# Two sixteen-head cross attentions of a four-layer decoder: the shift of the softmax from the leading bf16 parts, in row tiles

## The chip, the cores and the metric

The kernel runs on one core of a Trainium2 chip. The metric is the device time of one launch in microseconds (us). Every time below comes from the timed runs of the kernel before or from one profiled execution of it.

## The reference

A decoder of four layers works on `x` of shape (2, 512, 256), with a context of shape (2, 1024, 256). Each layer is self attention (or a recurrence, or retention), cross attention and a feed-forward part. The change concerns the cross attentions of layers 2 and 3, with 16 heads of 16 features, 512 queries and 1024 keys:

```
def _L2_xattn_ref(query, key, value, ..., key_padding_mask, attn_mask, Wq, bq, Wk, bk, Wv, bv, Wo, bo):
    ...
    scores = jnp.einsum('bhtd,bhsd->bhts', q, k) * scale
    scores = scores + attn_mask[None, None, :, :]
    scores = jnp.where(pad, -jnp.inf, scores)
    ...
    probs = jax.nn.softmax(scores, axis=-1)
    out = jnp.einsum('bhts,bhsd->bhtd', probs, v)
    return out @ Wo.T + bo
```

Layer 3 is the same without masks and biases. The mask of layer 2 is one (512, 1024) matrix of floats for all heads and both batch elements.

## The kernel before

The program is a row of stages, each with its own buffers, semaphores and a block for each engine; a stage begins when the one before has ended on all engines. `a2x` is the attention of layer 2, `a3x` that of layer 3; both call `narrow_attention_stage` (L2067). A projection stage ahead has written q and k to DRAM in three bf16 parts each (leading, middle, rest), whose sum has nearly the precision of float32.

The work goes by units: one batch element and a group of four heads, eight units in a stage. In a unit the six products of the parts are stacked to 96 contraction rows (`STACK`), so that one bf16 matmul gives scores of nearly float32 precision. The unit has two parts:

- *Chunks.* For each query tile of 128, each head and each half of the keys, one matmul (L2257) gives a 128x512 chunk in PSUM, of which VectorE takes the maximum over the keys: a plain reduction in a3x (L2400), in a2x a reduction that adds the float32 mask on the way (L2403). These are 32 chunks a unit, with two PSUM buffers of 512 (`chunk`). The maxima are reduced (L2421), turned by TensorE (L2268), split in three bf16 parts by VectorE (L2426 to L2433) and placed by DMA in three further contraction rows of q (L2204), beside three rows of ones in k.
- *Jobs.* For each tile of 128 keys and two heads, scores turned (keys on the partitions) minus the maximum come into `scores_T` (L2279), two buffers of 1024. In a2x, even key tiles get the mask by three bf16 matmuls against the identity (L2283), odd ones by an addition on VectorE into `masked` (L2412). ScalarE takes the exponential (L2379), TensorE multiplies with the values and a column of ones in column tiles of 32 (L2307) into `u`. At the unit's end ScalarE copies `u` (L2381), TensorE turns it (L2339) and VectorE divides (L2447, L2450).

The order on TensorE is written out by hand: chunks of the next unit (and ten of the one after) stand between the jobs of this one. Units run in loops over the head groups (`Fori`, L2235, L2354, L2384, L2462), two units in a turn. SyncE issues all loads in the order of its program. The stage `a0x` (`wide_attention_stage`, L457), which the change leaves alone, has eight heads of 64: its rows (L582) are two matmuls of 64 contraction rows each, with one reduction over 1024 elements (L726). `mask_stage` (L2822) prepares the mask parts and the padding row ahead of a2x.

## Time and profile before

| | us |
|---|---|
| median of 3 timed runs | 2957.84 (2949.81 to 2963.62) |
| profiled execution, its time | 2966.22 |
| its span, first to last instruction | 2964.4 |
| stage a2x | 393.75 |
| stage a3x | 261.99 |

The windows view, the first of the rows below that has stages, gives for each stretch its length, then the busy time of each engine with its number of instructions, TensorE's granted clock as a share of full speed, the busy share of the DMA engines and GB/s. The span is what the trace shows; 1.8 us of the execution lie outside it. A busy share counts the time in which an engine has an instruction under way. Matmul records overlap, as matmuls are pipelined: a 512-column matmul at full clock has a record of some 0.38 us and is followed by the next after 0.22.

### The profile page before, as it was taken

How to read it: one execution, taken by the hardware profiler on the slowest of the kernel's cores; microseconds unless marked ns; L12 is line 12 of the kernel's file. 1: busy time of each engine (PE TensorE's matmuls, PEld its weight loads, DVE VectorE, ACT ScalarE, POOL GpSimd, SP SyncE). 2: the span in 40 equal slices, each digit the busy share in tenths (PEclk: the TensorE clock that was granted, in tenths of full speed). 3: DMA queues.
4: the chain of work that ended last, by engine and by line, in shares of the span. 5: the costliest groups of instructions: out<-in, count | busy, mean ns of one | idle time of the engine just before them, and what ended most of it. 6: DMA issues, size and time to landing. Idle time of an engine off the chain costs nothing. (4 is left out here: it accounts for less than half of the span.)

```text
span 2964.4 us, 35664 instructions
## 1 busy us (share of the span) xinstructions
PE 2215.4 (75%) x11958; PEld 1048.9 (35%) x11958; DVE 1564.5 (53%) x2826; ACT 944.7 (32%) x1311; POOL 610.5 (21%) x540
## 2 busy tenths in 40 slices
PE   4778788897547766799567487887799693688854
PEld 2343322224424444555335122223444332322222
DVE  3543343425659998221433576674344425477757
ACT  2341133342224544122213133334110201345544
POOL 1000044440249999000101200000000101200013
PEclk8888899998768999799788699999899756789976
DMA  4502511100270500010441631200110000543000
GB/s 145 141 12 107 175 41 49 36 11 15 81 147 12 83 1 2 22 43 21 122 114 37 148 88 24 47 15 1 32 32 27 32 1 0 161 92 69 15 1 15
DMA packets 161134, 164.08 MB, mean 55 GB/s; under 512 B 14946, under 2 KB 131404, under 8 KB 160716
## 3 DMA queue, kind: packets, MB, share of 16 engines
q1 hardware_dynamic: 161000, 162.37, 21.3%
q8 instruction: 74, 1.21, 0.2%
q14 instruction: 60, 0.49, 0.1%
HBM read 108.97 MB, written 53.02 MB: 55 GB/s over the span
## 5 line engine op out<-in xcount | busy, mean ns | idle before, releaser
L2403 DVE CUSTOM_DVE_ANT_0 a2x_chunk<-a2x_chunk,mask 128x512 f32<-128x512 f32 x256 | 173.7, 703 | 80.9 <-PE a2x_chunk L2257 69.5
L726 DVE TENSOR_REDUCE a0x_row_most<-a0x_rows 128x2 f32<-128x1024 f32 x88 | 107.8, 1225 | 165.3 <-PE a0x_rows L582 165.3
L2400 DVE TENSOR_REDUCE a3x_chunk_maxima<-a3x_chunk 128x1 f32<-128x512 f32 x256 | 166.6, 689 | 40.4 <-PE a3x_chunk L2257 38.1
L1115 ACT ACTIVATE a1x_exp<-a1x_scores 128x1024 f32<-128x1024 f32 x128 | 124.1, 1021 | 174.9 <-PE a1x_scores L1046 174.9
L783 POOL TENSOR_TENSOR x_stream<-x_stream,feature_rows 128x256 f32<-128x256 f32 x40 | 27.9, 734 | 655.9 <-SPq L771 396.8
L2379 ACT ACTIVATE a3x_probs_T<-a3x_scores_T 128x1024 f32<-128x1024 f32 x128 | 128.7, 1025 | 101.8 <-PE a3x_scores_T L2279 101.6
L2257 PE MATMUL a2x_chunk<-a2x_ks,a2x_qs 97*128 (+1 forms) x256 | 105.5, 425 | 73.9 <-DVE a2x_chunk_maxima L2403 40.7
L1151 POOL TENSOR_TENSOR a1x_tree<-a1x_exp 128x1024 f32<-128x1024 f32 x64 | 150.4, 2351 | 43.1 <-ACT a1x_exp L1115 42.9
L561 POOL TENSOR_TENSOR a0x_pair_sums<-a0x_probs_T 128x1024 f32<-128x1024 f32 x48 | 112.7, 2347 | 186.7 <-ACT a0x_probs_T L679 186.7
L1084 DVE TENSOR_TENSOR a1x_exp<-a1x_exp,a1x_inverse_total 128x2048 f32<-128x2048 f32 x64 | 145.7, 2276 | 4.5 <-ACT a1x_inverse_total L1128 4.5
L679 ACT ACTIVATE a0x_probs_T<-a0x_scores_T 128x1024 f32<-128x1024 f32 x96 | 98.4, 1025 | 155.4 <-PE a0x_scores_T L608 155.3
L1035 PE MATMUL a1x_scores<-a1x_qs,a1x_ks 96*128 96x128 bf16 x1024 | 91.0, 241 | 71.7 <-ACT a1x_exp L1115 44.6
L2257 PE MATMUL a3x_chunk<-a3x_ks,a3x_qs 96*128 (+1 forms) x256 | 107.9, 425 | 33.8 <-DMA a3x_ks<-k_scr 16.6
L1094 DVE TENSOR_REDUCE a1x_most<-a1x_scores 128x128 bf16<-128x2048 f32 x43 | 98.5, 2292 | 44.7 <-PE a1x_scores L1035 44.7
L1046 PE MATMUL a1x_scores<-a1x_most,a1x_minus_ident 128*128 128x512 bf16 x256 | 71.3, 404 | 57.7 <-DVE a1x_most L1100 31.2
L2379 ACT ACTIVATE a2x_probs_T<-a2x_masked 128x1024 f32<-128x1024 f32 x64 | 67.6, 1057 | 138.3 <-DVE a2x_masked L2412 137.9
L1035 PEld LDWEIGHTS a1x_scores<-a1x_qs,a1x_ks 96*128 96x128 bf16 x1024 | 67.4, 108 | 120.1 <-ACT a1x_exp L1115 77.6
L604 PE MATMUL a0x_scores_T<-a0x_qs,a0x_ks 64*128 64x512 f32 x384 | 103.1, 615 | 5.4 <-ACT a0x_most_T L685 5.4
L2283 PE MATMUL a2x_scores_T<-mask_parts,ident_bf 128*128 128x512 bf16 x384 | 106.5, 386 | 0.0
L621 PE MATMUL a0x_u<-a0x_probs_T,a0x_vs 128*64 128x512 f32 x384 | 103.1, 617 | 0.0
L1368 DVE SCALAR_TENSOR_TENSOR x_stream<-m1f_op,m1f_cwe,x_stream 128x256 f32<-128x256 f32 x64 | 30.9, 483 | 134.0 <-PE m1f_op L1337 134.0
L2379 ACT ACTIVATE a2x_probs_T<-a2x_scores_T 128x1024 f32<-128x1024 f32 x64 | 64.5, 1020 | 93.0 <-PE a2x_scores_T L2283 93.0
(616 smaller groups left out, 4601.6 us busy)
## 6 DMA issues: line engine op xcount, KB each, us to landing
v_scr<-p0x_vout SPq DMA_DIRECT2D x24, 256.0 KB, 2.0
k_scr<-p0x_x SPq DMA_DIRECT2D x24, 256.0 KB, 2.3
a0x_ks<-k_scr SPq DMA_DIRECT2D x8, 768.0 KB, 5.2
a0x_vs<-v_scr SPq DMA_DIRECT2D x8, 768.0 KB, 4.8
m1f_ws<-in_L_ffn_w SPq DMA_DIRECT2D x24, 256.0 KB, 3.3
v_scr<-p1x_vout SPq DMA_DIRECT2D x16, 256.0 KB, 2.2
a1x_vs<-v_scr SPq DMA_DIRECT2D x16, 256.0 KB, 9.4
v_scr<-p2x_vout SPq DMA_DIRECT2D x16, 256.0 KB, 2.3
```

What stands on the lines that cost most here:

```text
L561: nc.gpsimd.tensor_tensor(pair[:, n // 2 % RP, :, :], pT[:, (n - 1) % R, :, :], pT[:, n % R, :, :], ALU.add).then_inc(paired, 1)
L604: nc.tensor.matmul(sT[:, n % 2, h, :], ks[hs, u % 3, kt * P:(kt + 1) * P], qs[hs, u % 3, :], start=True, stop=False, skip_group_check=True)
L726: nc.vector.tensor_reduce(rm[:, qt, :, c], row_psum(u, i)[:, :, :], AX.X, ALU.max).then_inc(row_most, 1)
L1035: mm = nc.tensor.matmul(sp_[:, g % 3, i, j, :], ks[0:96, h, kt * P:(kt + 1) * P], qs[0:96, h, qt * P:(qt + 1) * P], start=(j == 0), stop=F ...
L1084: nc.vector.tensor_tensor(ex[:, n % E, :, :], ex[:, n % E, :, :], rp[:, 0, :].unsqueeze(1).to_broadcast([P, H, P]), ALU.mult).then_inc(nor ...
L1115: nc.scalar.activation(ex[:, n % E, 8 * half:8 * half + 8, :], sp_[:, g % 3, :, :, :].rearrange("p i j q -> p (i j) q"), ACT.Exp).then_inc ...
L1151: nc.gpsimd.tensor_tensor(tree[:, :, :], e[:, 0:8], e[:, 8:16], ALU.add).then_inc(folded, 1)
L2257: mm = nc.tensor.matmul(cp[:, i % 2, o:o + n], at(qs, s, b, rows, h * T + qt * P, P), at(ks, s, b, rows, h * nkey + k0, n), start=True, st ...
L2283: mm = nc.tensor.matmul(sp_[:, i, o:o + n], core.ident_bf[:, :], full[2][:, part, kb // 2, :], start=False, stop=(part == 2))
L2379: nc.scalar.activation(dst, src, ACT.Exp).then_inc(expd, 1)
L2400: nc.vector.tensor_reduce(out, src.rearrange("p (h k) -> p h k", h=nh), AX.X, ALU.max).then_inc(chunk_max, 1)
L2403: nc.vector.tensor_tensor_reduce(out=src, in0=src, in1=full[0][:, qt, k0:k0 + n], scale=1.0, scalar=-3e38, op0=ALU.add, op1=ALU.max, accum ...
```

## The change

Both stages call a new `quad_attention_stage`. What it does:

- Chunks become *rows*: for each query tile, each half of the keys and each pair of heads, two matmuls with 16 contraction rows (17 in a2x, with the padding row), at partitions 32 times the head, from the leading bf16 parts of q and k alone, into `rows`, one PSUM buffer of two banks. In the first unit the two buffers of `scores_T` serve as well. VectorE reduces both heads' 512 keys in one instruction. In a2x the mask, rounded to bf16 in `mask_stage`, is added in PSUM by two matmuls against the identity.
- The shift is therefore not the exact maximum, only near it; it is rounded to bf16 and placed as one row (by ScalarE and one DMA) in place of three. The softmax does not change by it, as the same shift is in numerator and denominator.
- The leading parts are loaded once more, to their own partitions: 8 loads a unit, 16 in a2x.
- Scores, exponentials and values stay as they are, in half steps of two heads. The division is put off to the third key tile of the next unit. `lead` of 23 says how many rows TensorE is ahead.
- The code is written out for all eight units, without loops.

```
+def quad_attention_stage(core, name, nkey, q_parts, k_parts, v_scr, ao, keys_of, queries_of, lead, extra=0,
...
+    rows = []
+    for qt in range(QT):
+        k0, n = keys_of(qt)
+        for c in range(0, n, 512):
+            for pair in range(2):
+                rows.append((qt, pair, k0 + c, min(512, n - c), c // 512))
...
+    by_dve = [full is not None and kt % 2 == 1 for kt in range(KT)]
...
+        sT = st.ps("scores_T", [P, 2, 2, T])
+        rp = st.ps("rows", [P, 2, 512])
+        up = st.ps("u", [P, T])
+        mp = st.ps("turned", [P, 512])
...
+        def row_psum(r):
+
+            return rp if r >= NR or r % 3 == 0 else sT[:, r % 3 - 1]
...
+                def load_hi(u):
+                    g, b = units[u]
+                    for leading, buf in ((k_parts[2], kh), (q_parts[0], qh)):
+                        src = leading[:, b, :].rearrange("(d h) t -> h d t", d=16)
+                        for j in range(HG4):
+                            sp.dma_start(buf[32 * j:32 * j + 16, u % 2, :], src[HG4 * g + j]).then_inc(hi_in[u % 2], 16)
+                    if extra:
+                        for ap, buf in ((k_rows(g, b), kh), (q_rows(g, b), qh)):
+                            for j in range(HG4):
+                                sp.dma_start(buf[32 * j + 16:32 * j + 16 + extra, u % 2, :], ap[:, j, :]
+                                             ).then_inc(hi_in[u % 2], 16)
...
+                def place_shift(u):
+                    sp.wait_ge(shift_ready, u + 1)
+                    sp.dma_start(qs[K - 1:K, u % 2, :, :], shift[:, u % 2, :]).then_inc(shift_in[u % 2], 16)
+
+                load_hi(0)
+                load_stack(0)
+                for i in range(2):
+                    sp.dma_start(ks[K - 1:K, i, :, :], core.aps["ones_bf"][0:1, :, 0:nkey]).then_inc(ones_in, 16)
+                load_hi(1)
+                load_v(0)
+                place_shift(0)
...
+                load_stack(1)
...
+                for u in range(U):
+                    if u + 2 < U:
+                        sp.wait_ge(rowed, NR * (u + 1))
+                        load_hi(u + 2)
+                    if 1 <= u < U - 1:
+                        sp.wait_ge(scored, 2 * KT * u)
+                        load_stack(u + 1)
+                        sp.wait_ge(valued, KT * u)
+                        load_v(u + 1)
+                    if u + 1 < U:
+                        place_shift(u + 1)
...
+                def row(r):
+                    u, i = divmod(r, NR)
+                    qt, pair, k0, n, part = rows[i]
+                    if i == 0:
+                        pe.wait_ge(hi_in[u % 2], NHI * (u // 2 + 1))
+                    if r >= 3 and r < NR:
+                        pe.wait_ge(row_most, r - 2)
+                    elif r >= NR:
+                        pe.wait_ge(row_most, r)
+                    for j in range(2):
+                        h = 2 * pair + j
+                        hs = slice(32 * h, 32 * h + 16 + extra)
+                        mm = nc.tensor.matmul(row_psum(r)[:, j, 0:n], qh[hs, u % 2, qt * P:(qt + 1) * P],
+                                              kh[hs, u % 2, k0:k0 + n], start=True,
+                                              stop=(key_mask is None and full is None), skip_group_check=True)
+                    if key_mask is not None or full is not None:
+                        m0, mask = (k0, full[0][:, qt, k0:k0 + n]) if key_mask is None else key_mask(qt)
+                        for j in range(2):
+                            mm = nc.tensor.matmul(row_psum(r)[:, j, m0 - k0:m0 - k0 + mask.shape[1]],
+                                                  core.ident_bf[:, :], mask, start=False, stop=True,
+                                                  skip_group_check=True)
+                    mm.then_inc(rowed, 1)
...
+                    nc.tensor.transpose(mp[0:HG4 * QT, 0:P], mcol[:, u % 2, :], core.ident[:, :]
+                                        ).then_inc(most_turned, 1)
...
+                    if n and by_dve[(n - 1) % KT]:
+                        pe.wait_ge(masked, 2 * dve_before(n - 1) + half + 1)
+                    elif n:
+                        pe.wait_ge(expd, 2 * (n - 1) + half + 1)
+                    for j in range(2):
+                        h = 2 * half + j
+                        out = sT[:, half, j, :]
+                        mm = nc.tensor.matmul(out[:, 0:w], ks[0:K, u % 2, h, kt * P:(kt + 1) * P],
+                                              qs[0:K, u % 2, h, q0:q0 + w], start=True, stop=True,
+                                              skip_group_check=True)
+                        if full is not None and not by_dve[kt]:
+                            for part in range(3):
+                                mm = nc.tensor.matmul(out, core.ident_bf[:, :], full[2][:, part, kt // 2, :],
+                                                      start=False, stop=True, skip_group_check=True)
...
+                    for half in range(2):
+                        if n + 1 < N:
+                            score(n + 1, half)
+                        if half == 0 and n >= 1:
+                            value(n - 1)
+                        if kt == 2 and half == 1 and u:
+                            turn_u(u - 1)
+                        for _ in range(2):
+                            if done < min(2 * n + half + 1 + lead, U * NR):
+                                row(done)
+                                done += 1
+                        if turned < U and done >= min(NR * (turned + 1) + 1, NR * U) and (turned == 1 or kt > 2):
+                            turn_most(turned)
+                            turned += 1
...
+                def negate(u):
+                    act.wait_ge(most_turned, u + 1)
+                    if u >= 2:
+                        act.wait_ge(shift_in[u % 2], 16 * (u // 2))
+                    nc.scalar.mul(shift[:, u % 2, :], mp[0:HG4 * QT, 0:P], -1.0).then_inc(shift_ready, 1)
...
+                    nc.vector.tensor_reduce(rm[:, u % 2, at:at + QT + 1:QT, part], row_psum(r)[:, :, 0:n], AX.X, ALU.max
+                                            ).then_inc(row_most, 1)
...
-            narrow_attention_stage(core, "a2x", S, scr["q_scr"], scr["k_scr"], scr["v_scr"], ao, everything(S),
-                                   lambda kb: (0, T), extra=1, q_rows=ones_rows(a["ones_bf"], T, 1),
-                                   k_rows=lambda g, b: scr["pad_scr"][b], full=(mask, odd, mask_parts),
...
+                       scr["pad_scr"], mask, mask_bf)
+        ao = own.enter_context(nc.sbuf_tensor("ao2x", [P, NT, C], F32))
+        quad_attention_stage(core, "a2x", S, scr["q_scr"], scr["k_scr"], scr["v_scr"], ao, everything(S),
+                             lambda kt: (0, T), lead=23, extra=1, q_rows=ones_rows(a["ones_bf"], T, 1),
+                             k_rows=lambda g, b: scr["pad_scr"][b, 0:1], full=(mask_bf, odd, mask_parts),
...
-        narrow_attention_stage(core, "a3x", S, scr["q_scr"], scr["k_scr"], scr["v_scr"], ao, everything(S),
...
+        quad_attention_stage(core, "a3x", S, scr["q_scr"], scr["k_scr"], scr["v_scr"], ao, everything(S),
+                             lambda kt: (0, T), lead=23,
...
-def mask_stage(core, name, even, odd_src, pad, odd, mask_parts, pad_scr):
+def mask_stage(core, name, even, odd_src, pad, odd, mask_parts, pad_scr, mask, mask_bf):
...
+                nc.vector.tensor_copy(mask_bf[:, :, :], mask[:, :, :]).then_inc(rounded, 1)
                 for i in range(2):
                     dve.wait_ge(part, 2 * i + 1)
```

## Rows read from the trace of the kernel before

**Rows 1.** The page, part 1: busy us, share of the span, instructions.

```profile
PE 2215.4 (75%) x11958; PEld 1048.9 (35%) x11958; DVE 1564.5 (53%) x2826; ACT 944.7 (32%) x1311; POOL 610.5 (21%) x540
```

**Rows 2.** Windows: length; busy (x) of PE, PEld, DVE, ACT, POOL; PEclk; DMA share; GB/s.

```profile
1665.18:2058.93 393.75, 312.72 (x1448) 96.11 (x1448) 264.08 (x634) 135.67 (x138) 0.00 (x0) 0.90 0.21 41
2573.18:2835.17 261.99, 218.62 (x1064) 59.40 (x1064) 181.37 (x314) 134.16 (x138) 0.00 (x0) 0.91 0.31 61
1680.00:1714.00 34.00, 24.39 (x42) 4.27 (x41) 28.96 (x84) 0.00 (x0) 0.00 (x0) 0.50 0.30 48
560.00:620.00 60.00, 52.33 (x270) 14.16 (x266) 24.06 (x21) 23.62 (x27) 23.50 (x14) 1.00 0.08 24
2619.00:2622.00 3.00, 2.75 (x16) 0.69 (x8) 1.89 (x4) 1.07 (x3) 0.00 (x0) 0.94 1.06 367
```

**Rows 3.** Timeline of TensorE in a3x's steady part: start us, length us, engine, line.

```profile
2736.13 0.60 PE L2279 MATMUL a3x_scores_T<-a3x_qs,a3x_ks 99*128 x2
...
2738.16 1.06 PE L2307 MATMUL a3x_u<-a3x_probs_T,a3x_vs 128*32 128x512 f32 x8
...
2739.39 0.60 PE L2279 MATMUL a3x_scores_T<-a3x_qs,a3x_ks 99*128 x2
```

**Rows 4.** Timeline of a3x's last unit.

```profile
2809.88 1.04 PE L2279 MATMUL a3x_scores_T<-a3x_qs,a3x_ks 99*128 99x512 bf16 x4
2810.85 1.06 PE L2307 MATMUL a3x_u<-a3x_probs_T,a3x_vs 128*32 128x512 f32 x8
...
2823.77 3.90 ACT L2379 ACTIVATE a3x_probs_T<-a3x_scores_T 128x1024 f32<-128x1024 f32 x4 [0.27 <-PE a3x_scores_T L2279]
...
2827.94 3.91 ACT L2379 ACTIVATE a3x_probs_T<-a3x_scores_T 128x1024 f32<-128x1024 f32 x4 [0.27 <-PE a3x_scores_T L2279]
```

**Rows 5.** Timeline of a2x: three of eight u copies, and VectorE at the loop's end.

```profile
1760.68 0.59 ACT L2381 COPY a2x_u_sb<-a2x_u 128x512 f32<-128x512 f32 x1 [3.34 <-PE a2x_u L2307]
...
1802.61 0.59 ACT L2381 COPY a2x_u_sb<-a2x_u 128x512 f32<-128x512 f32 x1 [3.32 <-PE a2x_u L2307]
...
1809.39 0.70 DVE L2403 CUSTOM_DVE_ANT_0 a2x_chunk<-a2x_chunk,mask 128x512 f32<-128x512 f32 x1 [4.61 <-issue]
...
1852.65 0.59 ACT L2381 COPY a2x_u_sb<-a2x_u 128x512 f32<-128x512 f32 x1 [3.34 <-PE a2x_u L2307]
```

**Rows 6.** Timeline of the stages' beginnings: a2x's first scores, then a3x.

```profile
1714.83 0.63 PE L2279 MATMUL a2x_scores_T<-a2x_qs,a2x_ks 100*128 100x512 bf16 x1
...
2573.18 1.32 SPq L2179 DMA_DIRECT2D a3x_qs<-q_scr  x3
...
2605.20 0.19 DVE L2421 TENSOR_REDUCE a3x_maxima<-a3x_chunk_maxima 128x16 f32<-128x32 f32 x1
...
2605.95 0.28 DVE L2426 TENSOR_SCALAR a3x_max_parts<-a3x_turned 16x128 bf16<-16x128 f32 x1 [0.57 <-PE a3x_turned L2268]
...
2612.94 1.91 PE L2279 MATMUL a3x_scores_T<-a3x_qs,a3x_ks 99*128 99x512 bf16 x4
```

**Rows 7.** Timeline of a0x, its rows and their reductions.

```profile
568.40 1.23 DVE L726 TENSOR_REDUCE a0x_row_most<-a0x_rows 128x2 f32<-128x1024 f32 x1 [1.18 <-PE a0x_rows L582]
...
569.68 0.39 PE L582 MATMUL a0x_rows<-a0x_ks_bf,a0x_qs_bf 64*128 64x512 bf16 x2 [1.33 <-DVE a0x_row_most L726]
...
569.91 1.02 PE L604 MATMUL a0x_scores_T<-a0x_qs,a0x_ks 64*128 64x512 f32 x4
570.11 1.23 DVE L726 TENSOR_REDUCE a0x_row_most<-a0x_rows 128x2 f32<-128x1024 f32 x1 [0.49 <-PE a0x_rows L582]
```

**Rows 8.** Timeline of a0x's lead-in, VectorE alone.

```profile
353.22 2.34 DVE L726 TENSOR_REDUCE a0x_row_most<-a0x_scores_T 128x2 f32<-128x1024 f32 x2
```

**Rows 9.** The page, part 6: loads, KB each, median us to landing.

```profile
v_scr<-p0x_vout SPq DMA_DIRECT2D x24, 256.0 KB, 2.0
```

**Rows 10.** Lines in a2x, VectorE's mask addition: busy us, mean ns, idle before.

```profile
L2412 DVE TENSOR_TENSOR a2x_masked<-a2x_scores_T,x_norm_T 128x1024 f32<-128x1024 f32 x64 | 77.6, 1218 | 19.0 <-PE a2x_scores_T L2279 19.0
```

**Rows 11.** Timeline of the mask stage, VectorE's first subtraction.

```profile
1657.16 2.81 DVE L2863 TENSOR_TENSOR weights<-weights,mask_parts 128x2048 f32<-128x2048 f32 x1 [5.68 <-ACT mask_parts L2846]
```

## What the change should do to the time

> **What bounds the kernel now.** The page's busy shares come first: TensorE, the fullest engine, is busy for 75% of the span [rows 1]. No engine is full as a whole, so the answer lies in the stages. The change touches two, and the windows view cuts them out: a2x takes 393.75 us from SyncE's first issue to the last scaling, a3x 261.99 us [rows 2]. The rest of the program stays as it is, so the forecast is the new length of these two.
>
> Second, the timeline of a3x in its steady part. The scores of one key tile start at 2736.13, of the next at 2739.39 [rows 3]: 3.26 us a tile. TensorE has 2.6 of columns in it (four chunks and four scores of 0.217, values of 0.85), ScalarE two exponentials. When no chunks are left, in the last unit, four exponentials come in 4.17 us, 2823.77 to 2827.94 [rows 4]: 2.09 a tile. So it is not ScalarE that sets 3.26, but the search for the maximum, in which TensorE and VectorE hand PSUM to each other.
>
> Third, a2x: its u copies are 41.9 us apart, and every second time 50.0; in the 8.1 us more, VectorE stands still for 4.61 us that the profile puts down to "issue", at the end of its loop [rows 5]. The first scores of a2x start at 1714.83, 49.7 us into the stage, those of a3x 39.8 us in [rows 6].
>
> **The new row of maxima.** A unit has 16 rows (four query tiles, two pairs of heads, two halves of the keys), each two matmuls in row tiles and one reduction of 1024 elements, where 32 chunks of 512 were. The stage a0x has this pattern already: its two 64-row matmuls fit into the busy time of one (0.39 for x2), the reduction starts 0.43 after them and takes 1.23, and the scores' matmul comes 0.23 after the row's [rows 7]. It has one PSUM buffer for rows, and two reductions start 1.71 us apart at the closest (568.40 to 570.11). The new stage has one buffer too (`rp`; only the first unit also uses `scores_T`), so 1.71 is my floor for a row. With three buffers a0x's reductions come closer: two in 2.34, the last of them 1.21, so 1.13 apart [rows 8].
>
> **a3x, steady.** Each half step has two scores and one row, every second also a key tile's values. Scores to values: 0.97 for four scores (2809.88 to 2810.85) [rows 4], that is 0.10 above their columns, so 0.53 for two. Values to what follows: 1.00 (2738.16 to 2739.39 with a chunk of 0.23 between) [rows 3]. So from a row over scores and values to the next row TensorE needs 0.22 + 0.53 + 1.00 = 1.75, just above the floor; in the other half step 0.75, and the floor of 1.71 holds. Mean 1.73 a row, 3.46 a tile: 0.20 slower than now.
>
> **a3x, the sum.** Eight small loads at 0.44 (three take 1.32 [rows 6]) are 3.5; landing 2.0 [rows 9]; the big stacks come behind them in the queue: first row at 5.5. To the first reduction 0.7, 16 rows at 1.13 = 18.1: 24.3. The shift: from the maxima's last reduction to the use of the turned copy 0.75 [rows 6], negation 0.3, issue and landing 2.45, together 3.5; scores start at 27.8, 12.0 us sooner than now. With `lead` at 23 seven half steps do two rows and 98 do one: 112 x 1.73 = 193.8. Turning and scaling u hold up the row chain for some 0.8 in seven units (an estimate from the scaling's two operations and the turn): 5.6. The last 23 half steps have no rows: 11.5 x 2.09 = 24.0. Last copy, turn, scaling 2.7. The clock is at its lower level when scores start, now too, and 0.94 some 7 us later [rows 2]; I add 2.0. In all 27.8 + 228.1 = 255.9 against 262.0: 6.1 faster.
>
> **a2x, steady.** The mask comes into each row by two matmuls over the whole array: 0.22 + 0.10 for leaving row tiles + 0.43 = 0.75 of TensorE, and the reduction can start 0.97 after the row does. The row chain is then 0.05 + 0.97 + 1.21 = 2.23. Half an even key tile is eight matmuls, 1.74; half an odd one two, 0.43, and an addition of 1.22 on VectorE [rows 10]. Four half steps, counted from the odd tile's scores: scores to 0.43, values to 1.53, row to 2.28, its reduction from 2.50 to 3.71. Scores to 2.71; the next row waits for that reduction until 3.76 and ends at 4.51; VectorE adds the mask first and reduces it to 6.14. Scores to 6.25, values to 7.35, row to 8.10, reduced at 9.53. Scores to 9.84, row to 10.7. With 0.1 that carries over: 10.8 us, 2.71 a half step, 43.4 a unit. Now a unit has 41.9 [rows 5]. TensorE waits for only 1.0 of the 10.8: it becomes the bound.
>
> **a2x, the sum.** Sixteen loads 7.0 and landing 2.0: 9.0. The lead-in is bound by VectorE at 1.13 a row with the full clock and by TensorE at 1.5 (0.43 + 0.85 + 0.2) with half: 18.1 to 24; I take 21, because the clock was 0.50 in the lead-in with TensorE's gaps and rose once scores kept it busy [rows 2]. With 0.7 and 3.5 scores start at 34.2, 15.5 sooner. Then 105 half steps x 2.71 = 284.6, seven doubled rows x 2.2 = 15.4, seven turnovers x 1.1 = 7.7, 23 half steps at 6.6 for four = 38.0, end 4.4, half clock 2.5: 386.8. The two stalls of 8.1 us at the loop's end don't come up in it, since the new code is written out without a loop.
>
> **The mask stage** gets a cast of 4096 elements a partition on VectorE, ahead of a subtraction that starts at 1657.16 and takes 2.81 for 2048 [rows 11]. By that rate the cast takes 5.6; as it has one source I take less than half, and 0.3 us of delay behind ScalarE's cast, at most 3.5. The Trainium skill, "VectorE: DVE Perf Modes", lets a one-source operation within SBUF run two elements a cycle where a two-source one doesn't; no row here shows a cast of this size.
>
> **New waits, and what is behind them.** TensorE waits for each row's reduction before the next row; the next scores stand behind it, ScalarE behind those, with 1.4 us to spare a tile in a3x. ScalarE's negation waits for the turned maxima once a unit, in the same slack. SyncE issues 26 loads a unit in a2x, some 10 us in 43, and the shift row is ready half a unit before its use. All cost nothing as long as the half steps above are longer than 1.05.
>
> Sum: 393.7 - 387.1 = 6.6 in a2x with the mask stage, and 6.1: 12.7 us faster. The profiled run took 2966.22 us with 2964.4 of span; from the runs' median of 2957.84 the same difference gives **2945**. This measurement can tell about 0.5%, 14.8 us (2943), from no change; the forecast stands just inside that edge.
>
> **Tile switches** are the least sure term, 0.10 or 0.15 each by the rows. The Trainium skill, "TensorEngine Tiling (Array Packing)", Tiling Modes, says that a change of mode drains the engine; a row tile pair followed by a mask over the whole array changes it twice. By that rule the time is the forecast or worse, without it that of the first rival.
>
> **Rivals.**
> *Switches are free.* Six times 0.10 in four half steps, x 26.3 = 15.8 in a2x, 1.3 in a3x: 2928. For it: a0x goes from rows to scores in the columns' time [rows 7], though both are 64-row tiles.
> *Switches cost twice.* 15.8 more in a2x; in a3x 0.2 in 56 gaps: 2972, no measurable change.
> *Pairs of 32-row tiles don't overlap.* 0.22 on each of 224 rows is 49: 2994, slower. From 0.13 a row on it is slower by the measure. Against it: a0x's pairs [rows 7].
> *Code fetch.* If straight-line code stalls as the loop's end does, four stalls of 8.1 make it 2977 and slower. a0x, written out too, shows none.
> *The clock falls* in a3x, where TensorE waits 0.96 in every second gap. At the lower level a tile needs some 5.2: 56 x 1.7 = 95, 3040. For it: 0.50 in the lead-in with TensorE busy for 24.39 of 34. Against: a0x waits 1.33 before a row and holds 1.00 for 60 us [rows 2, 7]. The Trainium skill, "TensorE: Matmul & The Clock Gate", A second HAM failure mode, tells of a kernel whose small waits for PSUM made the clock swing; a0x differs from it.
>
> **Chances and range.** Forecast 0.46 (own range 2933 to 2958, 0.22 of it past the edge), free switches 0.21, dear switches 0.12, no overlap 0.12, fetch 0.05, clock 0.04. Faster 0.22 + 0.21 = 0.43; same 0.24 + 0.12 = 0.36; slower 0.21. The range 2922 to 2988 leaves out the clock, most of fetch, the upper part of no overlap and the tail of free switches, 0.19.
>
> **What would show it.** Reductions of 1024 elements at 1.22; in a3x 3.46 us from one key tile's scores to the next's; in a2x 10.8 for two tiles and u copies 43 to 45 apart with no 50; scores starting 28 us into a3x and 34 into a2x. Wrong would be: a pair of row matmuls busy for 0.6, mask matmuls more than 0.35 after their row, a granted clock under 0.95 past the lead-in, idle time put down to "issue".

## The result

The changed kernel takes 3053.05 us in the median of four runs (3048.18 to 3061.32), beside 2958.44 (2949.81 to 2963.62) for the kernel before on the same chip: a ratio of 1.0317, 95% interval 1.0288 to 1.0347. It is slower by 3%, outside the range and on the side that the prediction held least likely.

The windows view of the changed kernel, with the columns of [rows 2]: both stages, 20 us of a2x (lead-in, then first scores at 1692.08) and its steady part, then three stretches of a3x.

```profile
1656.86:2046.70 389.84, 338.72 (x1672) 105.11 (x1704) 232.57 (x216) 138.69 (x146) 0.00 (x0) 0.92 0.20 45
2561.98:2922.14 360.16, 302.15 (x1064) 49.24 (x1064) 161.91 (x152) 135.51 (x146) 0.00 (x0) 0.55 0.22 49
1680.00:1700.00 20.00, 15.08 (x44) 3.65 (x43) 9.40 (x10) 2.73 (x4) 0.00 (x0) 0.59 0.41 77
1700.00:2000.00 300.00, 266.90 (x1369) 86.46 (x1397) 192.66 (x179) 109.85 (x115) 0.00 (x0) 0.97 0.20 46
2590.00:2700.00 110.00, 91.96 (x298) 13.53 (x298) 51.41 (x46) 38.34 (x41) 0.00 (x0) 0.50 0.29 68
2720.00:2890.00 170.00, 156.48 (x513) 24.50 (x513) 77.80 (x73) 63.01 (x67) 0.00 (x0) 0.50 0.20 43
2900.00:2922.00 22.00, 19.40 (x120) 4.48 (x120) 1.22 (x4) 17.58 (x19) 0.00 (x0) 1.00 0.00 1
```

a2x went from 393.75 to 389.84 us, a3x from 261.99 to 360.16 [rows 2]. The sum of the two, +94.3, is the whole of the measured +94.6. In a3x the granted clock is 0.55: at the lower of TensorE's two levels (1.2 GHz) nearly throughout, and at 2.4 GHz only for some 10 us in the middle and when the last unit has no rows left. Note the busy columns beside it: TensorE is busy for 156.48 of 170 us and still at 0.50.

The timeline of a3x, first at half clock, then in the one short stretch at full clock before the last unit (2706.8 to 2717):

```profile
2807.18 0.61 PE L2600 MATMUL a3x_rows<-a3x_ks_hi,a3x_qs_hi 16*128 16x512 bf16 x2
2807.72 1.03 PE L2633 MATMUL a3x_scores_T<-a3x_qs,a3x_ks 97*128 97x512 bf16 x2
2809.11 0.60 PE L2600 MATMUL a3x_rows<-a3x_ks_hi,a3x_qs_hi 16*128 16x512 bf16 x2 [0.36 <-DVE a3x_row_most L2752]
2809.65 1.03 PE L2633 MATMUL a3x_scores_T<-a3x_qs,a3x_ks 97*128 97x512 bf16 x2
2810.61 1.94 PE L2656 MATMUL a3x_u<-a3x_probs_T,a3x_vs 128*32 128x512 f32 x8
2812.48 0.61 PE L2600 MATMUL a3x_rows<-a3x_ks_hi,a3x_qs_hi 16*128 16x512 bf16 x2
```

```profile
2708.83 0.39 PE L2600 MATMUL a3x_rows<-a3x_ks_hi,a3x_qs_hi 16*128 16x512 bf16 x2
2709.26 1.23 DVE L2752 TENSOR_REDUCE a3x_row_most<-a3x_rows 128x2 f32<-128x1024 f32 x1 [0.49 <-PE a3x_rows L2600]
2710.54 0.39 PE L2600 MATMUL a3x_rows<-a3x_ks_hi,a3x_qs_hi 16*128 16x512 bf16 x2 [0.79 <-DVE a3x_row_most L2752]
2710.97 1.23 DVE L2752 TENSOR_REDUCE a3x_row_most<-a3x_rows 128x2 f32<-128x1024 f32 x1 [0.49 <-PE a3x_rows L2600]
```

A tile (two rows) takes 5.30 us from 2807.18 to 2812.48, with every matmul longer and one wait of 0.36. At full clock the same rows are 1.71 apart, pair busy 0.39, reduction 0.43 after it: the floor of the prediction [rows 7].

The timeline of a2x: a row and the same row four half steps on, then three u copies, answering to [rows 5].

```profile
1851.09 0.39 PE L2600 MATMUL a2x_rows<-a2x_ks_hi,a2x_qs_hi 17*128 17x512 bf16 x2
1851.41 0.60 PE L2606 MATMUL a2x_rows<-mask_bf,ident_bf 128*128 128x512 bf16 x2
...
1861.80 0.39 PE L2600 MATMUL a2x_rows<-a2x_ks_hi,a2x_qs_hi 17*128 17x512 bf16 x2
```

```profile
1765.09 0.59 ACT L2723 COPY a2x_u_sb<-a2x_u 128x512 f32<-128x512 f32 x1 [1.29 <-PE a2x_u L2656]
...
1808.16 0.59 ACT L2723 COPY a2x_u_sb<-a2x_u 128x512 f32<-128x512 f32 x1 [1.29 <-PE a2x_u L2656]
...
1851.22 0.59 ACT L2723 COPY a2x_u_sb<-a2x_u 128x512 f32<-128x512 f32 x1 [1.29 <-PE a2x_u L2656]
```

Four half steps take 10.71 us, units are 43.07 apart each time, and no 50 is among them.

### The profile page after: what moved, and what is told of

Read it like the earlier page. It is cut to its first block and busy times, and to the rows that moved or that the text cites. A ratio compares the mean times of both kernels' runs of the same rounds, so it can differ in the third digit from the quotient of the medians.

```text
span 3051.6 us, 33480 instructions
## 1 busy us (share of the span) xinstructions
PE 2315.4 (76%) x12181; PEld 1041.6 (34%) x12214; DVE 1517.9 (50%) x2247; ACT 948.7 (31%) x1327; POOL 610.7 (20%) x540
## 5 line engine op out<-in xcount | busy, mean ns | idle before, releaser
L2752 DVE TENSOR_REDUCE a3x_row_most<-a3x_rows 128x2 f32<-128x1024 f32 x118 | 144.6, 1225 | 169.5 <-PE a3x_rows L2600 159.3
L2752 DVE TENSOR_REDUCE a2x_row_most<-a2x_rows 128x2 f32<-128x1024 f32 x118 | 144.4, 1224 | 118.2 <-PE a2x_rows L2606 112.9
L2633 PE MATMUL a3x_scores_T<-a3x_qs,a3x_ks 97*128 97x512 bf16 x256 | 121.4, 578 | 12.5 <-ACT a3x_probs_T L2711 10.2
L2656 PE MATMUL a3x_u<-a3x_probs_T,a3x_vs 128*32 128x512 f32 x512 | 112.1, 965 | 0.1
L2600 PE MATMUL a3x_rows<-a3x_ks_hi,a3x_qs_hi 16*128 16x512 bf16 x236 | 70.4, 593 | 43.0 <-DVE a3x_row_most L2752 30.2
```

The source lines that it names most:

```text
L2633: mm = nc.tensor.matmul(out[:, 0:w], ks[0:K, u % 2, h, kt * P:(kt + 1) * P], qs[0:K, u % 2, h, q0:q0 + w], start=True, stop=True, skip_gro ...
L2656: mm = nc.tensor.matmul(up[hs, q0:q0 + w], vs[:, u % 2, kt, hs], pT[:, n % R, h, 0:w], start=(kt == 0), stop=True, skip_group_check=True)
L2752: nc.vector.tensor_reduce(rm[:, u % 2, at:at + QT + 1:QT, part], row_psum(r)[:, :, 0:n], AX.X, ALU.max).then_inc(row_most, 1)
```

## The experiments

All keep a2x as in the change unless said; "stage" is from ScalarE's table load at its beginning to the last scaling. Ratios are to the kernel before, with 95% intervals.

**The loss is in a3x alone** (e1). a3x by the narrow stage again:

```
-        quad_attention_stage(core, "a3x", ..., lead=23, ...)
+        narrow_attention_stage(core, "a3x", ..., k_rows=ones_rows(a["ones_bf"], S), ...)
```

> The a2x stage is rebuilt as in the change, the a3x stage is the narrow one of before. Every theory that puts the loss into a3x alone expects the gain of a2x and the mask cast and nothing else: -3.9 us from the stage, +1 from the mask stage, so 2952 to 2957 us where the kernel before takes 2958, with a3x at 262 us and a granted clock near 0.9 in it. A theory in which the loss is not in a3x (a longer program, code fetch, the layout of memory) expects over 2970.

2961.54 us beside 2965.32, ratio 0.9994 (0.998 to 1.0008). The windows view of a3x:

```profile
2567.24:2829.01 261.77, 218.67 (x1064) 59.35 (x1064) 181.45 (x314) 134.07 (x138) 0.00 (x0) 0.91 0.30 61
```

The loss is all in a3x. The 3.9 us that a2x gains in the profiles (389.7 for 393.75) are too few to show in the timed runs.

**Is it the waits for the one row buffer?** Four runs put matmuls in their place. e2 issues each score matmul of the second half twice, e4 three times; e5 adds two over 16 rows ahead of each; e3 doubles the pairs of rows.

```
-                        mm = nc.tensor.matmul(out[:, 0:w], ks[0:K, ...], qs[0:K, ...], ...)
+                        for _ in range(2 if full is None and half == 1 else 1):      # e2; 3 in e4
+                            mm = nc.tensor.matmul(out[:, 0:w], ks[0:K, ...], qs[0:K, ...], ...)
...
-                    for j in range(2):
+                    for j in list(range(2)) * (2 if full is None else 1):            # e3, in row()
```

> Only a3x differs from the changed kernel: its two score matmuls of the second half (97 rows tall, 512 columns) are each issued twice, the second time over the first with the same result. That is 2 x 0.21 = 0.43 us more for TensorE a tile at full clock, inside the 0.96 us that it waits for the row buffer. Theory A (the waits for the one row buffer keep the clock at its lower level, any matmul that fills them lifts it): clock 0.85 to 1.00 in a3x, stage 256 to 268 us, kernel 2948 to 2962. Theory B (the 16-row matmuls of the rows count little with whatever decides the clock, tall ones count): the same as A here. Theory C (the clock in a3x is tied to something else, as the start of the stage): clock stays at 0.5 and the stage grows from 360 to about 370 or more, since the half clock makes TensorE the bound. Theory D (the rows themselves are dear, the clock is only a companion): clock rises and the stage is still over 275.

> Only a3x differs from the changed kernel: each pair of 16-row row matmuls is issued twice, the second pair over the first with the same result, 0.22 us more a row at full clock and 0.44 a tile, much as in the doubled scores. Theory A: clock 0.85 to 1.00, rows 1.95 us apart at full clock (1.73 + 0.22), so up to 3.9 a tile, 56 tiles x 3.9 = 218 and the stage 275 to 285 us, kernel about 2965 to 2980. Theory B: clock stays near 0.55, a tile 5.29 + 0.87 = 6.2 us at most, stage 380 to 410 us, kernel 3075 to 3100. Theory D expects the same as B without the clock's help: a stage over 380.

> In a3x each of the two score matmuls of the second half is issued three times, over itself, all 97 rows tall: two extra pairs, 0.86 us of TensorE a tile at full clock. With one extra pair the granted clock was 0.62 in the stage instead of 0.55, in stretches of TensorE busy for 20.00 of 20 us still 0.50. Theory B (what counts is tall matmuls, the 16-row ones of the rows give little): another pair lifts the clock further, to 0.75 to 1.00, and the stage to 256 to 320 us. Theory A (idle time alone): TensorE is already without idle time at half clock, so nothing more is to be had: the clock stays at 0.50 to 0.62 and the stage grows by up to 0.86 us a tile, 56 x 0.86 = 48, to 380 to 410 us.

> The same number of extra matmuls in the same place with the same columns as in the tall fill (two extra pairs a tile, before the real score matmuls of the second half, which write over them), but over 16 rows of the stack in place of 97. Theory B: the clock stays at 0.50 to 0.58 and the stage takes 390 to 420 us (360 and up to 56 x 0.86 = 48 more). If height does not matter and only the time in which TensorE has work does, this run shows the clock and the stage of the tall fill within a few per cent.

| | stage a3x, us | clock | ratio |
|---|---|---|---|
| changed kernel | 360.2 | 0.55 | 1.0317 |
| e2, one tall pair | 361.1 | 0.62 | none; 3062.46 us beside 2965.32, single runs from 3016.85 to 3070.75 |
| e3, rows twice | 412.2 | 0.53 | 1.0498 (1.0474 to 1.0523) |
| e4, two tall pairs | 309.8 | 0.83 | 1.0151 (1.0124 to 1.0178) |
| e5, two short pairs | 338.1 | 0.76 | 1.0278 (1.0253 to 1.0303) |

e2 fits none of its theories: a little more clock, and no time gained. Theory A, that any matmul in the waits lifts the clock, falls: e3 has more work in it than the changed kernel and a lower clock, in the range of theory B but 2 us above its stage. The windows view of e2 and of the later e11 shows 2690 to 2720 of each trace:

```profile
2690.00:2720.00 30.00, 30.00 (x96) 5.71 (x94) 13.36 (x13) 10.87 (x12) 0.00 (x0) 0.50 0.25 57
```

```profile
2690.00:2720.00 30.00, 22.78 (x137) 5.23 (x133) 20.10 (x20) 16.47 (x19) 0.00 (x0) 1.00 0.28 63
```

In e2 TensorE is busy for 30.00 of 30 us at half clock; in e11 it stands still for a quarter of them at full clock. But e5 goes against theory B as I put it: its fill is 16 rows tall and lifts the clock too, to 0.76 where the tall one gives 0.83. Nor are the waits without effect. The windows view of e4 and of e5, each after its clock has risen:

```profile
2670.00:2835.00 165.00, 157.49 (x885) 44.57 (x883) 109.49 (x104) 85.65 (x94) 0.00 (x0) 1.00 0.29 57
```

```profile
2705.00:2848.00 143.00, 137.43 (x774) 31.66 (x772) 95.67 (x89) 75.40 (x83) 0.00 (x0) 1.00 0.34 65
```

The rows are still 16 tall here and the clock holds at 1.00 for 165 and 143 us, with TensorE idle for under 5% of them. So two pairs in the waits hold the full clock once it is up, but do not bring it up early: both runs are at 0.50 for their first 100 us or more, TensorE busy for all of the last 20 of them.

**Height or time?** e6 and e7 both undo the row tiles of a3x, so the two matmuls of a step follow each other. e6 surrounds the 16 rows of q with zeros up to 128 and clears the buffers first; e7 puts all heads on the same 16 partitions.

```
+        qh = st.sb("qs_hi", [P, 2, HG4, T], BF16)      # e6; [16, 2, HG4, T] and kh alike in e7
...
-                        hs = slice(32 * h, 32 * h + 16 + extra)
+                        hs = slice(0, P)                # e6; slice(0, 16) in e7
```

> In a3x the row tiles are undone: the row matmul of a head takes all 128 rows of the array, its 16 rows of q with zeros around them, so the two of a step follow each other instead of running side by side; nothing else is added, and the buffers are cleared once at the start of the stage (some us). Theory B: the clock rises to 0.85 to 1.00; a row is then up to 0.22 us longer than 1.73 us, 112 x 1.95 = 218 and with 34 of lead-in and 28 of last unit 265 to 285 us for the stage, kernel 2960 to 2980. Theory A (the waits for the one row buffer matter, not the height): the clock stays near 0.55, the row is longer by 0.43 at half clock, and the stage is 385 to 410.

> As the padded rows, the row tiles of a3x are undone, but the row matmuls stay 16 rows tall: all four heads lie on the same 16 partitions, so the two of a step follow each other. Between this run and the padded one (stage 303 us, clock 0.89) only the height differs (16 rows or 128); between this run and the changed kernel (360 us, 0.55) only that the two matmuls of a step follow each other. Theory B (height counts): clock 0.50 to 0.60, stage 385 to 410 us. Theory C (the time counts in which columns stream, and two matmuls side by side stream in half the time): clock 0.80 to 0.92, stage 295 to 320 us.

The windows view of the stage, e6 and then e7:

```profile
2564.55:2872.80 308.25, 222.72 (x1064) 55.03 (x1064) 161.91 (x152) 134.35 (x146) 5.29 (x3) 0.89 0.25 57
```

```profile
2563.82:2975.61 411.79, 361.42 (x1064) 52.91 (x1064) 162.44 (x152) 135.70 (x146) 0.00 (x0) 0.53 0.19 43
```

The same 1064 matmuls with the same columns in the same order: 308 us at 0.89 with 128 rows, of which 5.3 are the clearing on GpSimd, 412 at 0.53 with 16 (ratios 1.0154, 1.013 to 1.0177, and 1.0514, 1.0499 to 1.0529). Height decides here, and theory C of this pair (that the time of the columns counts) falls. The forecast of e6 missed all the same: 265 to 285 us for the stage. The timeline of e6 has a longer wait before its row than the changed kernel at half clock, and keeps its clock:

```profile
2691.21 0.60 PE L2607 MATMUL a3x_rows<-a3x_ks_hi,a3x_qs_hi 128*128 128x512 bf16 x2 [0.89 <-DVE a3x_row_most L2759]
```

**Row tiles again, taller.** Side by side as in the change, with zeros up to 64, 32 and 24 rows, cleared by VectorE in some 1.2 us ahead of the first load.

```
-        qh = st.sb("qs_hi", [P, 2, T], BF16)
+        qh = st.sb("qs_hi", [P, 2, 2, T], BF16)        # e11: a plane for each pair of heads
...
-                        hs = slice(32 * h, 32 * h + 16 + extra)
+                        hs = slice(64 * j, 64 * j + 64)  # e11; slice(32 * h, 32 * h + 32) in e12, + 24 in e13
```

> In a3x the two row matmuls of a step still run side by side, in two row tiles of 64 rows in place of 16: the 16 rows of a head with 48 rows of zeros on the side of q, cleared once by VectorE at the start of the stage (some 3 us). Work in time is that of the changed kernel, 1.73 us a row and 3.46 a tile at full clock; only the number of array rows under the stream differs. Theory B (the height of the row matmuls decides, 64 + 64 rows count about as the 128 that followed each other): clock 0.85 to 1.00, stage 6 + 27 + 56 x 3.5 + 28 = 257 us, 252 to 272 with stretches at half clock, kernel 2945 to 2965 beside 2960. Theory H (only matmuls over the full array, one after the other, lift it): clock 0.50 to 0.60, stage 355 to 370 us, kernel 3050 to 3060.

> As the 64-row tiles, but 32 rows for each head, 16 of them zeros: 64 rows under the stream of a step. Theory B with a smooth dependence on height: a little more than the 32 rows of the changed kernel, clock 0.53 to 0.70, stage 320 to 366 us. If it is the tile that the array opens for a matmul and not the rows filled: the same as the changed kernel, 0.55 and 355 to 366 us. If any zeros that fill a tile do it: 0.85 or more and 252 to 272 us.

> As the 32-row tiles (0.83, stage 289 us), but the row matmuls take 24 rows, 16 of q and 8 zeros. If the dependence is a slope: clock about 0.65 to 0.75 and 310 to 335 us. If 16 rows lie just under what is needed: as 32 rows, 0.80 to 0.85 and 285 to 300. If a row group has to be filled: as 16 rows, 0.55 and 355 to 365.

The windows view of the stage, e13, e12, e11:

```profile
2565.06:2863.02 297.96, 223.74 (x1064) 43.79 (x1064) 162.85 (x156) 134.85 (x146) 0.00 (x0) 0.79 0.27 59
```

```profile
2573.81:2864.13 290.32, 214.03 (x1064) 43.35 (x1064) 162.85 (x156) 134.82 (x146) 0.00 (x0) 0.83 0.28 60
```

```profile
2572.71:2858.55 285.84, 209.02 (x1064) 43.27 (x1064) 163.30 (x156) 134.94 (x146) 0.00 (x0) 0.85 0.28 61
```

Ratios 1.013 (1.0104 to 1.0157), 1.0124 (1.0105 to 1.0143), 1.0093 (1.0075 to 1.0111). Eight rows of zeros, in matmuls of unchanged time, take 62 us off the stage; the next eight 8, the next 32 another 4.5. These are single profiled executions; the intervals of the timed runs tell 16 rows from the rest clearly, 24 from 32 not at all and 32 from 64 hardly. Theory B is borne out in its direction and theory H falls, and so does the even slope that I gave as one way for 24 and 32 rows. But the stages of e11 and e12 (285.8 and 290.3 us) are longer than the 252 to 272 that I gave for a clock of 0.85 and more; e13 comes closest, with 298.0 for 285 to 300 and 0.79 for 0.80 to 0.85. The zeros are on the side of q; on the side of k, the added rows of e12 and e13 are zeros too, while those of e6 and e11 hold the keys of other heads, which meet the zeros of q.

**Does the half clock keep itself?** fp32 matmuls of the identity fill a3x's lead-in: after each of its first 16 rows and before its first scores (e8, e9, e10), in e14 to e16 before the first row too.

```
+                def warm():
+                    nc.tensor.matmul(up[:, 0:P], core.ident[:, :], core.ident[:, :], start=True, stop=True,
+                                     skip_group_check=True)
...
                     row(done)
+                    warm()
```

> Only the fills of the lead-in of a3x, the steady state as in the changed kernel. Theory F (the lower clock keeps itself: once up the stage would stay up): clock over 0.85 and the stage 254 to 275 us. Theory G (the steady state itself does not hold the clock, as where the changed kernel had it at 1.00 for some 10 us and lost it): the clock is up for the first tens of us at most, 0.50 to 0.70 in the mean, stage 330 to 362 us.

> One extra pair of score matmuls a tile and the fills of the lead-in. One extra pair alone gave 0.62 and 361 us. Theory F: over 0.85 and 254 to 275 us. Theory G: one extra pair may lie near what holds the clock (it was at 1.00 for 27 us in one stretch), so 0.60 to 0.85 and 280 to 350 us, with a wide scatter from run to run.

> The tall fill (two extra pairs of score matmuls a tile) and, in the lead-in of a3x, one fp32 matmul of the identity with itself (128 columns) after each of the first 16 rows and seven between the turning of the first maxima and the first scores, into the buffer of u that is not in use yet. The tall fill alone had 0.50 for the stage's first 105 us and 1.00 after them, with 3.57 us a tile. If filled idle time lifts the clock, it is up before the first scores: 28 + 56 x 3.57 + 28 = 256 us for the stage at 1.00, 252 to 270 with what is left of the rise, kernel 2943 to 2962, beside 2958 for the kernel before: the same or up to 0.5% faster. If the lead-in has nothing to do with when it rises: 310 us as without, kernel 3005.

e9: 366.3 us, 0.54, 1.031 (1.0291 to 1.0328). e10: 371.3 us, 0.60, 1.0354 (1.0323 to 1.0385). e8: 340.6 us, 0.75, 1.0243 (1.0219 to 1.0267), single runs from 3021.14 to 3097.07. Around the first scores the clock was up for some 7 us in each and fell back when the steady state began, as theory G has it, but the stages of e9 and e10 are longer than its ranges (330 to 362 and 280 to 350). e8 missed: it is worse than e4 without the lead-in's fills, and its runs lie 76 us apart. In e9 it stays at 0.50 under the fills between the rows, with TensorE busy all the time, and rises in the fills after the last row. With 16-row rows these fills did not bring the rise forward.

**What is left with the clock up?**

> The 64-row tiles, whose stage had its first 55 us at half clock, with TensorE kept at work in the lead-in of a3x: twenty fp32 matmuls of the identity before the first row, one after each of the first 16 rows, seven before the first scores, all into the idle buffer of u. If that lifts the clock before the steady state: the first tiles take 3.5 in place of 5.3 us, some 10 tiles x 1.8 = 18 us less, stage 262 to 270 us, kernel 2965 to 2975. If not (in the 16-row version the same fills raised it for 7 us only): 285 us as without them.

> As the run before, and one extra pair of score matmuls a tile in the steady state of a3x. If the half-clock stretches of 3 to 10 us in the steady state come from TensorE's remaining waits for the row buffer: clock 0.93 to 1.00, 56 x 3.5 = 196, with 28 + 28 + 5 some 257 us, 254 to 264, kernel 2948 to 2960, the same as before or up to 0.4% faster. If they have another cause: 262 to 275.

> As the run before, with 64-row tiles in a2x too and twenty fp32 fills before its first row. a2x took 389.8 us, 28 of them a lead-in with 1.51 us a row at half clock where VectorE alone would take 1.22: up to 16 x 0.3 = 5 us to be had if its clock is up by then. Steady state of a2x at 0.97 already, so nothing there: a2x 384 to 391 us, kernel 2943 to 2958, at best 0.6% faster than before.

e14: 291.1 us, 0.87, 1.0093 (1.0071 to 1.0114). e15: 288.1 us, 0.91, 1.008 (1.0064 to 1.0096). e16: 2975.69 us, 1.0036 (1.0019 to 1.0053), a3x 288.2, a2x 379.4. All three missed in a3x (e14 by 6 us beyond even its second case), and e16 in its total, while its a2x is 5 us better than its range: e15 has the clock of the kernel before [rows 2] and takes 26 us longer than it. The timeline of e11 at full clock, TensorE with ScalarE's negation first, then VectorE's last reduction of two units; then two u copies of the kernel before:

```profile
2761.00 0.39 PE L2610 MATMUL a3x_rows<-a3x_ks_hi,a3x_qs_hi 64*128 64x512 bf16 x2 [0.79 <-DVE a3x_row_most L2762]
...
2761.32 0.60 PE L2643 MATMUL a3x_scores_T<-a3x_qs,a3x_ks 97*128 97x512 bf16 x2
...
2761.85 1.07 PE L2666 MATMUL a3x_u<-a3x_probs_T,a3x_vs 128*32 128x512 f32 x8
...
2762.85 0.39 PE L2610 MATMUL a3x_rows<-a3x_ks_hi,a3x_qs_hi 64*128 64x512 bf16 x2
...
2764.66 0.39 PE L2610 MATMUL a3x_rows<-a3x_ks_hi,a3x_qs_hi 64*128 64x512 bf16 x2 [0.88 <-DVE a3x_row_most L2762]
...
2765.30 0.27 ACT L2727 ACTIVATE a3x_shift<-a3x_turned 16x128 bf16<-16x128 f32 x1 [4.03 <-PE a3x_turned L2627]
...
2766.52 0.60 PE L2643 MATMUL a3x_scores_T<-a3x_qs,a3x_ks 97*128 97x512 bf16 x2 [1.26 <-ACT a3x_probs_T L2721]
...
2768.05 0.39 PE L2610 MATMUL a3x_rows<-a3x_ks_hi,a3x_qs_hi 64*128 64x512 bf16 x2
...
2771.63 0.39 PE L2610 MATMUL a3x_rows<-a3x_ks_hi,a3x_qs_hi 64*128 64x512 bf16 x2
...
2773.34 0.39 PE L2610 MATMUL a3x_rows<-a3x_ks_hi,a3x_qs_hi 64*128 64x512 bf16 x2 [0.79 <-DVE a3x_row_most L2762]
```

```profile
2764.55 0.19 DVE L2768 TENSOR_REDUCE a3x_most<-a3x_row_most 128x16 f32<-128x32 f32 x1
...
2794.75 0.19 DVE L2768 TENSOR_REDUCE a3x_most<-a3x_row_most 128x16 f32<-128x32 f32 x1
```

```profile
2701.87 0.59 ACT L2381 COPY a3x_u_sb<-a3x_u 128x512 f32<-128x512 f32 x1 [3.46 <-PE a3x_u L2307]
...
2730.76 0.59 ACT L2381 COPY a3x_u_sb<-a3x_u 128x512 f32<-128x512 f32 x1 [3.47 <-PE a3x_u L2307]
```

Rows are 1.85 us apart over a half step with values (2761.00 to 2762.85) and 1.71 over one without (2771.63 to 2773.34): some 3.57 a tile where I had 3.46. The 1.85 are 0.32 from the row to the scores, 0.53 to the values and 1.00 to the next row. Once a unit it is 3.39 (2764.66 to 2768.05): ScalarE's negation stands ahead of the next exponentials in its program, so ScalarE idles 4.03 us for the turned maxima, and the next scores wait 1.26 for the exponentials behind. A unit is 30.20 us, with the clock at 1.00, beside 28.89 before. From the first maxima, 23.8 us into the stage of the changed kernel, seven such units and the last one's 30.4 (e11, some 3 us of them at the lower clock) make 265.6: an estimate of a3x with next to no half clock in its steady state, 3.6 slower than before.

**What is a2x worth?** a2x with 64-row tiles and twenty fp32 matmuls before its first row (e17), or with those matmuls alone (e18); a3x by the narrow stage.

> a2x with 64-row tiles and twenty fp32 matmuls of the identity before its first row; a3x by the narrow stage of before. a2x as in the run that had both stages so: 379 us in place of 393.7, a3x 262, mask stage +1: 2961 - 14.7 + 1 = 2947 us, a ratio of 0.993 to 0.997.

> As the run before, but a2x keeps the row tiles of the change (17 rows for a head). If the filled start alone lifts the clock in the lead-in: a2x 383 to 386 us or less, kernel 2951 to 2955. If 17 rows keep it down in the lead-in as 16 rows did in a3x: 389 to 392 us, the same as the run with a2x of the change alone (ratio 0.9994).

The windows view of a2x in the run with the change's a2x alone, in e18 and in e17, each followed by 20 us around its lead-in (in e18 and e17 the first scores, at 1697.95 and 1687.76, fall into them):

```profile
1662.43:2052.13 389.70, 343.26 (x1704) 105.20 (x1704) 232.57 (x216) 138.62 (x146) 0.00 (x0) 0.92 0.20 45
1677.00:1697.00 20.00, 16.95 (x45) 2.58 (x45) 14.90 (x13) 0.27 (x1) 0.00 (x0) 0.50 0.10 29
```

```profile
1668.82:2051.52 382.70, 335.48 (x1712) 111.53 (x1744) 231.14 (x216) 138.60 (x146) 0.00 (x0) 0.95 0.20 46
1684.00:1704.00 20.00, 13.52 (x53) 3.90 (x53) 11.60 (x12) 2.04 (x3) 0.00 (x0) 0.83 0.41 89
```

```profile
1657.31:2036.99 379.68, 330.98 (x1712) 111.24 (x1744) 232.95 (x220) 138.62 (x146) 0.00 (x0) 0.97 0.20 46
1672.00:1692.00 20.00, 13.13 (x49) 3.44 (x49) 13.20 (x13) 0.89 (x2) 0.00 (x0) 0.87 0.35 79
```

e17: 2949.24 us beside 2961.43, ratio 0.9961 (0.9947 to 0.9975). e18: 2953.74 us, 0.9969 (0.9956 to 0.9982). Both beat the kernel before by some 0.3 to 0.4%, and the changed one by far; between the two the intervals don't decide. In the profiles the filled start brings the first scores from 35.2 to 29.1 us into the stage (30.4 in e17, which clears its buffers first). The rest of the stage is some 4 us shorter with the taller rows (349.2 after the first scores in e17, 353.6 in e18, 354.5 without either), in one execution of each, which the timed runs don't confirm.

## Why the prediction was wrong

- **a2x: right.** Four half steps 10.71 (10.8), a unit 43.07 (43.4), first scores 35.2 us in (34.2), stage 389.84 (386.8). The two stalls of 8.1 us are gone. That is 3 us more than forecast, and the terms that were short are the lead-in, whose half clock gives 1.51 us a row as reckoned and lasts through it, and what lies around the steady part.
- **Pairs overlap, switches cost about what I took:** 0.39 for two matmuls of 17 rows; from a row to its mask 0.32. The rivals of free switches, dear switches, no overlap and code fetch are all out.
- **The mask's cast**, in the timeline of the mask stage with ScalarE's cast ahead of it and the first subtraction behind it, and ScalarE's cast in the kernel before,

```profile
1646.31 1.90 ACT L3180 CAST mask_parts<-weights 128x2048 bf16<-128x2048 f32 x1 [4.45 <-PEq L274]
1646.33 2.29 DVE L3193 CAST mask_bf<-mask 128x4096 bf16<-128x4096 f32 x1 [3.75 <-PEq L274]
1648.54 3.12 DVE L3197 TENSOR_TENSOR weights<-weights,mask_parts 128x2048 f32<-128x2048 f32 x1
```

```profile
1655.23 1.90 ACT L2846 CAST mask_parts<-weights 128x2048 bf16<-128x2048 f32 x1 [4.47 <-PEq L274]
```

  takes 2.29 us, two fifths of what the subtraction's rate gives. The subtraction starts 2.23 us after ScalarE's cast, beside 1.93 before [rows 11]: the 0.3 of the forecast. It is itself 0.3 longer, and the mask stage grows by 0.6, from 9.96 to 10.56. The Trainium skill, "VectorE: DVE Perf Modes", Mode 2×_2P, gives a one-source operation within SBUF two elements a cycle and a two-source one not; the trace agrees, with 4096 elements in 2.29 us beside 2048 in 2.81 [rows 11].
- **a3x, the size of the steady state: short.** A unit was to take 16 x 1.73 + 0.8 = 28.5 and takes 30.20 at full clock: 16 x 1.78 = 28.5 for the rows and 1.7 for the turn. With the rest that is 265.6 for 255.9, which turns the 6.1 of gain into 3.6 of loss before the clock comes in. Two steps failed here. The 1.75 over scores and values counted 0.22 from a row to its scores, without the 0.10 for leaving row tiles that the sum for a2x has; it is 0.32, and 1.85 in all. And the wait of the negation was called hidden in ScalarE's slack, which it isn't.
- **a3x, the clock: this step failed.** "The clock falls" was a rival at 0.04 with 5.2 us a tile and 95 us of loss; it came with 5.30 and, from the estimate above, 360.2 - 265.6 = 94.6. The forecast itself had 2.0 us for the lower clock, after the first scores only. The price of the rival was right and its chance wrong. What I set against it was that a0x waits 1.33 before a row and holds 1.00 [rows 2, 7]. The comparison looked at the waits, and at nothing else of the rows: those of a0x are 64 rows tall, those of a3x 16. With rows as tall as a0x's, and the same waits, a3x is at 1.00 in most of its steady state (e11). That a2x did not fall fits, though no run tests it: behind each of its rows stand two mask matmuls over 128 rows. The waits are not innocent: with 16-row rows the full clock held for 165 us where they were filled (e4) and for some 10 us where they weren't. The failed step is thus that waits of this size leave the clock alone whatever stands between them. The Trainium skill, "TensorE: Matmul & The Clock Gate", A second HAM failure mode, gives small waits for PSUM as the cause of a swinging clock. The trace agrees in that filling them helps (e4), but they are there at 0.85 (e11) as at 0.55, and between those two the measurement puts the difference on the height.

Open: why the 16-row fill of e5 lifts the clock (in it, as in e2 and e4, TensorE hardly waits at half clock; that its matmuls stand in no row tiles is not enough, as those of e7 don't either and e7 stays at 0.53); why the clock rises when it does in e4 and e5; why eight rows of zeros do nearly all; and why 64-row rows have the lower clock for most of the first 73 us of a3x (e11), or with the fills of e14 for most of the 41 us after the first 36. e11 to e13 also clear two buffers at the stage's beginning, which the changed kernel doesn't; that this plays a part is not excluded by a run of its own. A filled start in the narrow a3x, which has 51 us at the lower clock itself, wasn't tried.

## What to carry to other kernels

Before thin matmuls replace tall ones, look at what else keeps TensorE's clock up in that stretch, and compare with a stretch that is alike in height, not only in waits; where the clock drops, try padding the contraction with zeros. In row tiles it cost no matmul time here (0.39 us a pair with 16 rows and with 64) and 1.2 us of clearing, and was worth 62 to 74 us. A busy share near 100% doesn't tell the clock (e2): read the granted clock of the stage first. And price a rival that would cost 95 us with more care than one of 5, however unlikely it seems.

## What was unexpected in the hardware

- TensorE busy for 30.00 of 30 us at the lower clock (e2), and for 22.78 of 30 at the full one (e11).
- With 16-row rows and two extra pairs in the waits, 165 us without a break at the full clock (e4), after 100 us without one at the lower.
- The same 1064 matmuls in the same order, in row tiles: 0.55 with 16 rows, 0.79 with 24, 0.83 with 32, 0.85 with 64, the added rows being zeros on the side of q.
- With 16-row rows and fills, executions of one kernel lay up to 76 us apart (e8), the longest with a mean granted clock of 0.829 over the whole kernel and the shortest with 0.854.
